# Router logits with the tokens' columns as the loaded operand, and the last two groups routed one slot sooner, in an adaLN block with linear attention and a mixture of experts

## What is computed

```python
h = layernorm(x) * (1 + ca) + sa
x = x + ga * attention(h)             # 16 heads of 16, phi = elu + 1, causal linear attention
h = layernorm(x) * (1 + cb) + sb      # sb, cb, gb: one row of 256 for each of the 4 batches

logits = h @ w_router.T               # 8 experts
gates = softmax(logits); two best experts for each token
position in the expert = running count over the tokens; at most 1280 are kept for each expert
hidden = silu(h @ w_gate.T)
y = sum over the two experts of gate * (hidden @ w_down[e].T)
x = x + gb * y
```

## Time and profile before

| what | value |
|---|---|
| median of 3 runs | 863.83 us (863.52 to 989.26) |
| profiled execution, its own time | 863.09 us |
| span from first to last instruction of it | 861.1 us |
| outside the span | 2.0 us |
| TensorE busy | 790.2 us, 92% |
| VectorE, ScalarE, GpSimd busy | 585.6, 488.7, 472.5 us |

### The profile page before, as it was taken

How to read it: one execution, slowest core, us unless ns; L and a number is a source line. 1 busy time by engine, 2 the same in 40 slices (tenths; PEclk the granted TensorE clock), 3 DMA queues, 4 the chain that set the end, 5 groups by cost and what they waited for, 6 DMA issues and landing times.

```text
span 861.1 us, 24360 instructions
## 1 busy us (share of the span) xinstructions
PE 790.2 (92%) x9388; PEld 647.2 (75%) x9388; DVE 585.6 (68%) x1753; ACT 488.7 (57%) x1001; POOL 472.5 (55%) x579
## 2 busy tenths in 40 slices
PE   5899999999999999999999999722999999999993
PEld 4676777777777777777777777511999999999993
DVE  4666677777776877867777767770566767767662
ACT  5656665766756756667657665421555555554541
POOL 2202345664664675665656645465356656656654
PEclk9999999999999999999999999955999999999997
DMA  5579913232332233323222212223466676677553
GB/s 195 175 229 284 310 19 125 84 91 100 84 114 90 86 111 95 83 97 71 66 86 64 52 50 58 48 78 120 102 155 130 135 167 133 146 158 156 122 91 37
DMA packets 71425, 99.00 MB, mean 115 GB/s; under 512 B 7810, under 2 KB 52866, under 8 KB 71320
## 3 DMA queue, kind: packets, MB, share of 16 engines
q1 hardware_dynamic: 38744, 53.93, 22.7%
q0 software_dynamic: 21760, 31.66, 16.9%
q10 hardware_dynamic: 10816, 11.96, 4.4%
HBM read 46.84 MB, written 63.36 MB: 128 GB/s over the span
## 4 chain that ended last, share of the span: by engine, by line
PE 73%; POOL 9%; issue 6%; ACT 6%; DVE 4%; DMA 2%; ACTq 0%; POOLq 0%; SPq 0%; DVEq 0%
PE SCW L1523 13%; PE PJ L1365 7%; PE SCW L1538 7%; PE MD L1538 6%; PE SCW L1305 6%; PE MD L1338 5%; PE SCW L1269 5%; PE PJ L1375 3%; PE SCW L1289 3%; POOL slot_rows L495 3%; PE MD L1279 3%; ACT N L671 2%; POOL rs L539 2%; POOL hT L532 2%; DVE Sm L919 2%
## 5 line engine op out<-in xcount | busy, mean ns | idle before, releaser
L495 POOL DMA_INDIRECT slot_rows<-Hrow,sloti x128 | 127.5, 996 | 141.4 <-PE SCW L1295 57.5
L919 DVE TENSOR_TENSOR Sm<-SCW,tri 128x1024 f32<-128x1024 f32 x128 | 150.8, 1220 | 71.5 <-PE SCW L1269 69.9
L601 POOL DMA_INDIRECT out<-EX,desti x80 | 128.2, 1602 | 31.8 <-issue 31.8
L1365 PE MATMUL PJ<-hT,w_qkv 128*128 128x512 f32 x384 | 109.8, 419 | 2.4 <-POOL hT L532 2.4
L1365 PEld LDWEIGHTS PJ<-hT,w_qkv 128*128 128x128 f32 x384 | 69.8, 190 | 25.5 <-issue 7.2
L671 ACT ACTIVATE N<-X,nb,rs 128x256 f32<-128x256 f32 x128 | 66.3, 591 | 27.4 <-POOL nb L541 27.4
L1305 PE MATMUL SCW<-Sm,VA 128*17 128x128 f32 x2048 | 80.6, 275 | 0.0
L667 ACT ACTIVATE EX<-PJ 128x512 f32<-128x512 f32 x64 | 37.9, 592 | 66.7 <-PE PJ L1365 66.7
L1269 PE MATMUL SCW<-QM,KT 32*128 32x256 f32 x1024 | 73.3, 400 | 0.8 <-ACT OTs L789 0.5
L1338 PE MATMUL MD<-w_og,ATs 128*128 128x256 f32 x256 | 72.4, 405 | 0.5 <-ACT ATs L778 0.5
L827 ACT ACTIVATE VA<-SCW 128x512 f32<-128x512 f32 x80 | 47.8, 598 | 41.0 <-PE SCW L1523 40.5
(11 more groups left out here) (189 smaller groups left out, 1767.1 us busy)
## 6 DMA issues: line engine op xcount, KB each, us to landing
Hrow<-slot_rows SPq DMA_DIRECT2D x32, 516.0 KB, 4.1
slot_rows<-erow ACTq DMA_DIRECT2D x1, 10400.0 KB, 46.6
X<-x SPq DMA_DIRECT2D x16, 512.0 KB, 5.6
out<-X SPq DMA_DIRECT2D x16, 512.0 KB, 2.9
Hrow<-mod_rows SPq DMA_DIRECT2D x16, 512.0 KB, 7.9
QT<-slot_rows SPq DMA_DIRECT2D x8, 516.0 KB, 3.7
slot_rows<-Hrow,sloti POOLq DMA_INDIRECT x128, 2.8
N<-wd SPq DMA_DIRECT2D x4, 512.0 KB, 4.2
```

Of the source, the lines that this page charges most:

```text
L495: pool.indirect_dma_start(xe, bass.IndirectOffsetOnAxis(sloti[:, par, k, t:t + 1], 0), Hrow[:, par, t, :], None, bounds_check=SLOTS - 1, o ...
L601: pool.indirect_dma_start(out, bass.IndirectOffsetOnAxis(desti[s % 2][:, a:a + 1], 0), Ys[s % 2][:, a, :], None, bounds_check=TOK - 1, oob ...
L919: dve.tensor_tensor(o.rearrange("p c (k w) -> p c k w", k=2), SCW[:, 2 * pair:2 * pair + 2, :].rearrange("p k (c w) -> p c k w", c=DC), tr ...
L1365: last = mm(PJ[m % 2][:], w_qkv[:, wp, cc, m * P:(m + 1) * P], hT[:, hp, cc, :], start=(cc + i == 0), stop=(cc == DC - 1 and i == len(SPLI ...
```

## The change

There are three parts.

- **Logits of all groups.** `h2T` becomes the loaded operand (128 x 128 for each of 4 tiles and 2 halves), and `w_r` with its 32 columns streams. The result has tokens on the partitions, so `logit_rows`, `lgT`, `lg` and both copies of ScalarE go away, and `choose` reads the logits from PSUM.
- **Group 14** has its statistics in slot 60, its normalisation in slot 61, its columns and logits in slot 62, `choose` in slot 63 and `place` in slot 64.
- **Group 15** is normalised in two pieces (three tiles, then one) and routed at once in a function `last_group`. In both groups the rows to send come from `h2T`: TensorE transposes it back (`rows_back`) and ScalarE copies it to `Hrow` (`rows_kept`), in place of VectorE's 16 scalings. The sends of GpSimd are listed anew.

The diff, cut (the same name `last_group` appears in several engines; `weights` is the block with the two `Exp` and the copy that stood at the end of ScalarE's slot; `columns_scaled` scales a range of columns as L745 did):

```diff
+        last_lg = KR[:, 0:GT * 32].rearrange("p (t w) -> p t w", t=GT)
+        last_pos = KR[:, 256:256 + GT * E].rearrange("p (t e) -> p t e", t=GT)
...
-            late = {TILES - 3: "pick", TILES - 2: "place", TILES - 1: "columns", TILES: "pick", TILES + 1: "place"}
+            late = {TILES - 3: "pick", TILES - 2: "place", TILES - 1: "pick", TILES: "place"}
             if n in late:
-                return (n + 1) // 4 - 2 if n != TILES + 1 else GROUPS - 2, late[n]
-            return n // 4 - 2, (("columns", "first", "second", "place")[n % 4] if n // 4 - 2 != GROUPS - 2 else None)
+                return GROUPS - 3 + (n - TILES + 3) // 2, late[n]
+            return n // 4 - 2, ("columns", "first", "second", "place")[n % 4]
...
+                    if g >= GROUPS - 2:
+                        pool.wait_ge(rows_out, 2 * (g - GROUPS + 2) + 2)
                     pool.tensor_tensor(idle[:, 5:6], mhalf[:, 0:1], mhalf[:, 0:1], ALU.add).then_inc(rested, 1)
-                    if g == GROUPS - 1:
-                        pool.wait_ge(last_rows, 1)
...
                     departure(GROUPS - 3)
-                    send_row(0, 0)
+                    send_row(0, 0, 1)
+                    pool.wait_ge(on_full, TILES - 1)
+                    send_row(0, 1, 1)
                     pool.wait_ge(knt_full, TILES)
-                    send_row(0, 1)
-                    pool.wait_ge(state_full, TILES)
-                    send_row(1, 0)
+                    send_row(1, 0, 1)
+                    pool.wait_ge(at_full, TILES - 1)
+                    send_row(1, 1, 1)
                     pool.wait_ge(sent[0], 128 * (GROUPS // 2 - 1))
                     number(GROUPS - 2)
+                    pool.wait_ge(state_full, TILES)
+                    send_row(2, 0, 1)
+                    pool.wait_ge(op_full, TILES - 1)
+                    send_row(2, 1, 1)
+                def last_deviations(t0, t1, part):
+
+                    ts = slice(t0, t1)
+                    pool.wait_ge(vpe2, GROUPS - 1 + part)
+                    pool.tensor_tensor(rs2[:, ts], vp2[:, ts], mhalf[:, ts], ALU.pow).then_inc(pow2, 1)
+                    pool.wait_ge(pow2, GROUPS - 1 + part)
+                    pool.tensor_tensor(nb2[:, ts], nm2[:, ts], rs2[:, ts], ALU.mult).then_inc(rstd2, 1)
+
                 if n == TILES:
+                    last_deviations(0, GT - 1, 1)
                     pool.wait_ge(on_full, TILES)
-                    send_row(1, 1)
-                    pool.wait_ge(at_full, TILES)
-                    send_row(2, 0)
-                    pool.wait_ge(op_full, TILES)
-                    send_row(2, 1)
-                if leaving and gn > GROUPS:
-                    send(2 * q)
-                    if q == 0:
-                        send(1)
+                    send_row(3, 0, 1)
+                    send_row(3, 1, 1)
+                    departure(GROUPS - 2)
+                    send_row(0, 0, 0)
+                    last_deviations(GT - 1, GT, 2)
+                    send_row(0, 1, 0)
+                    for t in range(1, GT):
+                        for k in range(2):
+                            send_row(t, k, 0)
+                    pool.wait_ge(sent[1], 128 * (GROUPS // 2 - 1))
+                    number(GROUPS - 1)
+                    departure(GROUPS - 1)
+                    for t in range(GT):
+                        for k in range(2):
+                            send_row(t, k, 1)
...
+                if q == 1 and gn == GROUPS - 1:
+                    deviations(rs2, vp2, nm2, nb2, vpe2, pow2, rstd2, G)
...
+            def last_norm(t):
+
+                act.wait_ge(rstd2, GROUPS - 1 + (1 if t < GT - 1 else 2))
+                act.wait_ge(h_lo, 2 * GROUPS)
+                normalise(N1[:, t, :], t, (GROUPS - 1) * GT + t, rs2, nb2, n2_ready)
+
+            def columns_scaled(cidx, cols, full):
+
+                act.wait_ge(h2t_full, full)
+                act.wait_ge(col2_done, 1)
+                act.activation(h2T[:, cidx, cols], PJ[cidx][:, cols], ACT.Identity,
+                               scale=saca2[:, DC + cidx:DC + cidx + 1],
+                               bias=saca2[:, cidx:cidx + 1]).then_inc(h2t_done, 1)
+
+            def rows_kept(g, half):
+
+                late = g - GROUPS + 2
+                act.wait_ge(sent[g % 2], 128 * (GROUPS // 2 - 1))
+                act.wait_ge(back_full, 2 * late + half + 1)
+                act.activation(Hrow[:, g % 2, 2 * half:2 * half + 2, 0:D],
+                               PJ[half * late][:].rearrange("p (t d) -> p t d", t=2), ACT.Copy).then_inc(rows_out, 1)
...
+            def last_group():
+
+                for t in (0, 1):
+                    last_norm(t)
+                act.wait_ge(at_full, TILES)
+                act.activation(ATs[:].rearrange("p c i -> p (c i)"), MA[:, 0:D], ACT.Copy).then_inc(at_done, 1)
+                last_norm(2)
+                act.wait_ge(lg_full, GROUPS - 1)
+                act.wait_ge(back_full, 2)
+                for cidx in range(DC):
+                    columns_scaled(cidx, slice(0, 3 * P), 2 * (GROUPS - 1) + cidx + 1)
+                last_norm(3)
+                for cidx in range(DC):
+                    columns_scaled(cidx, slice(3 * P, 4 * P), 2 * GROUPS + cidx + 1)
+                for half in range(2):
+                    rows_kept(GROUPS - 1, half)
+                weights(GROUPS - 1)
...
-                if routed and step in ("first", "pick"):
-                    act.wait_ge(lgt_full, g + 1)
-                    act.activation(lgT[:], PJ[1][:, 0:P], ACT.Copy).then_inc(lgt_done, 1)
...
-                if routed and step in ("first", "pick"):
-                    take(lg, lg_ps[:, :, 0:E], lg_full, g)
...
+                if n == TILES - 2:
+                    act.wait_ge(lg_full, GROUPS - 2)
+                    for cidx in range(DC):
+                        columns_scaled(cidx, slice(0, GW), 2 * (GROUPS - 2) + cidx + 1)
                 if n == TILES - 1:
-                    columns_out()
...
+                of = (last_lg if g == GROUPS - 1 else lg_ps)[:, :, 0:E]
+                if k > 0:
+                    dve.wait_ge(route, NR * g + k)
+                else:
+                    dve.wait_ge(lg_full, g + 1)
                 if k == 0:
-                    dve.wait_ge(taken, g + 1)
-                else:
-                    dve.wait_ge(route, NR * g + k)
-                if k == 0:
-                    done(dve.tensor_reduce(lmax[:], lg[:], AX_X, ALU.max))
+                    done(dve.tensor_reduce(lmax[:], of, AX_X, ALU.max))
                 elif k == 1:
-                    done(dve.tensor_tensor(lp[:], lg[:], wide(lmax[:]), ALU.subtract))
+                    done(dve.tensor_tensor(lp[:], of, wide(lmax[:]), ALU.subtract))
...
+            def last_deviations(t0, t1, part, between):
+
+                ts = slice(t0, t1)
+                dve.wait_ge(n2_ready, 4 * (GROUPS - 1))
+                dve.wait_ge(bn2, 4 * (GROUPS - 1) + t1)
+                for t in range(t0, t1):
+                    dve.bn_aggr(mv2[:, t, :], st2[:, t, :]).then_inc(ag2, 1)
+                between()
+                dve.wait_ge(ag2, 4 * (GROUPS - 1) + t1)
+                dve.tensor_scalar(nm2[:, ts].unsqueeze(2), mv2[:, ts, 0:1], -1.0, None, ALU.mult)
+                dve.tensor_scalar(vp2[:, ts].unsqueeze(2), mv2[:, ts, 1:2], LN_EPS, None, ALU.add).then_inc(vpe2, 1)
+
+            def last_group():
+
+                normalise_heads(TILES, lambda: None, lambda: None)
+                for k in range(9):
+                    place(GROUPS - 2, k)
+                add_out(TILES)
+                dve.wait_ge(x1_done, TILES)
+                row_stats(TILES - 1, GT - 1)
+                last_deviations(GT - 1, GT, 2, lambda: None)
+                for k in range(13):
+                    choose(GROUPS - 1, k)
+                for k in range(9):
+                    place(GROUPS - 1, k)
...
+                if n == TILES - 4:
+
+                    dve.wait_ge(x1_done, n)
+                    row_stats(n - 1, GT - 1)
+                    dve.wait_ge(bn2, n)
+                    ln_tail(st2, mv2, vp2, nm2, ag2, vpe2, GROUPS - 1)
+                if n == TILES - 1:
+                    dve.wait_ge(x1_done, n)
+                    row_stats(n - 1, 2)
+                    last_deviations(0, GT - 1, 1, between)
...
-                if n == TILES - 1:
-
-                    dve.wait_ge(mb_in, 32)
-                    dve.wait_ge(n2_ready, 4 * (GROUPS - 1))
-                    dve.wait_ge(sent[0], 128 * (GROUPS // 2 - 1))
-                    for t in range(GT):
-                        dve.tensor_tensor(Hrow[:, 0, t, 0:D], N2[:, t, :], MB[:, BATCH - 1, 2, :],
-                                          ALU.mult).then_inc(h2_scaled, 1)
-                    for t in range(GT):
-                        dve.wait_ge(h2_scaled, 4 * (GROUPS - 2) + t + 1)
```

(69 more changed lines are left out.)

145 lines of the change are left out of this document (52 added, 93 removed).

## The result

The changed kernel takes 879.08 us (median of 4 runs, 874.38 to 883.75), the kernel before 867.33 in the same comparison (4 runs, 863.52 to 989.26): ratio 1.0158, 95% interval 1.0114 to 1.0201, both formed without the disturbed run of before (989.26), which is why the ratio isn't that of the two medians. It is slower, by 1.1 to 2.0%: clear of no change by its interval, while the 2% that the forecast set as its bar lies at the very end of the interval. The profiled execution took 874.38 us, 11.29 more than that of before.

A forecast was written before the change was run, and what follows sets the result against it. TensorE was taken to bound stage one, and VectorE's small steps then GpSimd's sends the stretch between stages. The profiled 863.09 us plus 14.8 for stage one less 2.7 at the end gave 875.2 us, range 866 to 882.

The forecast's parts named there:

- The forecast's own case: Whole kernel: each group's logits cost +1.0 to +1.35 us, the end changes by -4 to -1; chance 0.58.
- Stage one: TensorE's full stretch: 14 groups at 1.17 us, less 1.6 absorbed, add 14.8 us (12.8 to 20.2).
- The pair of load and product: New logits on TensorE: 0.115 us for each of 16 pairs, 1.84 us a group.
- Rival A: New logits: loads hide, 25 to 60 ns a pair, total 860 us, not slower; chance 0.14.
- rival B: New logits: load and stream serial, 0.139 us a pair, 880.6 us, or 883.3 without end gain; chance 0.12.
- What is absorbed: Stage one: TensorE's waits for GpSimd's low part of `hT`, in 7 groups, absorb 1.6 us in all.
- `choose` reads PSUM, not `lg`: VectorE's `choose` in stage one: its 32 elements cost the same within some 0.05 us.
- Rival D: Stage one: ScalarE's removed copies release TensorE by up to 0.58 us a group, total 867.1; chance 0.07.
- Slot 62: TensorE gets eight transposes (1.1 us) and group 14's logits (1.84) from slot 63, 2.9 us in all.
- 3.2 us sooner: Between the stages: GpSimd's first send of group 14 can start at 567.3, before 570.53.
- The end's gain: Between the stages: group 14 is routed and sent sooner, its sends done about 579.1; gain 2.7 us.
- Rival C: Between the stages: group 15's routing or the wait for deviations replaces the sends, no gain, 877.9; chance 0.09.

The follow-up runs named there:

- Experiment 1: The kernel before with only the new form of the logits, in all 16 groups: 876.27 us, ratio 1.0128 to the kernel before.
- experiment 4: The changed kernel with 128, 96, 64 and 32 columns streamed for a group's four tiles instead of 32, groups 0 to 14: 876.83 us, ratio 1.0119.
- 3: The changed kernel with 8 router columns streamed for each load instead of 32, in groups 0 to 14: 878.0 us, ratio 1.0133.
- 5: The changed kernel with the store of group 15's `X` rows issued behind the first loads of stage two: 874.16 us, ratio 1.0105.
- 8: The changed kernel with that store late and group 15's gates held back until the last logits are done: 877.62 us, ratio 1.0145.
- 2: The changed kernel with the old logits in groups 0 to 14, so the new end alone: 865.0 us, ratio 0.9984 to the kernel before.
- 6: The changed kernel with old logits in groups 0 to 14 and the late store of group 15's `X` rows: 862.2 us, ratio 0.9966.
- 11: The changed kernel with old logits in groups 0 to 14, late store, and tile 63's deviations behind the 114th send: 862.6 us, ratio 0.999.
- 9: The changed kernel with eight small additions more on GpSimd ahead of the last two sends of group 13: 876.69 us, one run.
- 10: The changed kernel with the last send of group 13 moved behind the first send of group 14: 875.66 us, one run.
- 7: The changed kernel with tile 63's deviations on GpSimd ahead of group 14's first send, not behind it: 880.66 us, ratio 1.018.

## Why the prediction was right, and where two of its terms were not

The time forecast was 875.2 us for the profiled execution, which took 874.38; the median of the first comparison is 879.08, inside 866 to 882. The forecast's own case (a group +1.0 to +1.35) came true in stage one. In the end (-4 to -1) it did not. Stage one added 11.4 us where 14.8 was forecast, and the end gave back 0.1 where 2.7 was forecast: two misses of 3.4 and 2.6 us cancel. That the sum is right to 0.8 us is luck; the main cost and its size are not.

**The pair of load and product** was taken as 0.115 us and is 0.112 (0.111 and 0.113 with other streams). A group was forecast at 1.17 us with the transpose taken off. It is 1.13 in the routed slot, less 0.06 in the slot behind it, 1.07: 15.1 us for 14 groups, where 16.4 was forecast. Experiment 1 gives the same with nothing else changed. L1236 of the earlier trace rows, halved for the clock, gave 0.106; the loads' 0.83 ns a column of the earlier trace rows gave 107 ns. The Trainium skill, page "TensorE: Matmul & The Clock Gate", section "LDWEIGHTS (loading the stationary operand)", whose rule made it 1.71 us, is within 5% of the 1.79 measured. The Trainium skill, section "Back-to-back issue gap" of the same page, gives the 60 cycles, which made 0.4 us, for a product by itself and says that they count no load; here, with a load for each product, it was 1.78 us with 8 columns and 1.80 with up to 128.

**Rival A** (the loads hide) is refuted by the same rows, and **rival B** (load and stream in series) by experiment 4: in series, an average of 80 columns streamed would have taken longer than 32, by L1338's 1.04 ns a column some 0.05 us a pair, 0.8 us in 16. It took 0.01 more.

**What is absorbed** was mis-sized: 1.6 us forecast, 3.0 measured (3.74 less the transpose's 0.75); another 0.7 came by the start and by steps of chance. The step that failed is "it shows in 7 groups, six at 0.16 or 0.17 us as in the earlier trace rows and the first at 0.64". The mechanism and the six groups were right, but the wait really costs 0.43 us each. The seventh could not absorb anything: it stands ahead of the first routed logits and is still 0.64 us in the changed kernel. A row's idle time counts from the modelled end of the matmul before it, which lies well behind the time at which the next could have started: from the first piece to the next product it was 1.91 us before and is 1.50 after, 0.41 less for a wait shown as 0.16. The slots' distances give the true size. The rest, 0.42 us in three slots, is a case of "`choose` reads PSUM, not `lg`; its 32 elements cost the same within some 0.05 us": VectorE's second step got 0.46 us shorter there, as shown with the result.

**Rival D** (missing cover of ScalarE's copies) would have given back up to 0.58 us a group. The routed slots grow by 1.13, and the slots behind that hold neither the wait for `hT` nor `w_og` give back 0.05 or 0.06, which the transpose explains. Nothing is left for the copies.

**Slot 62** grew by 2.30 us, not 2.9; the first send of group 14 starts 31.74 us after the scores of slot 61, forecast 31.5 (567.3 - 535.76), before 34.77. So "3.2 us sooner" was 3.0. This part held. In experiments 3, 4, 5 and 8, with the same list on GpSimd, that send comes at 31.04 to 31.10: the changed kernel's execution has a gap of 0.64 us in front of the gate that they lack.

**The end's gain** was 2.7 us by forecast and 0.1 measured. The step that failed is "Now it is 0.99 for the first, 1.6 for the deviations with their waits, and seven at 0.97 + 0.30". From the first send to the row numbers of group 15 it took 592.99 - 578.90 = 14.09 us, not 11.8. The deviations with their wait cost 1.12 (1.6 forecast), the sends 1.28 each as forecast, and in addition there is the pause of 3.28 us. The hitch before the same send in the kernel before, 1.53 us less the usual 0.30, was part of the 11.3 us that I read, and I let it vanish in the new sum where I should have carried it. It did not vanish, it grew by 1.75. Why it is there isn't known (see below). **Rival C** had this price (2.7 us), and its place, but not its cause: the deviations came early enough (wait 0.27 us), and group 15 was routed 2.5 us before its turn, where 0.8 was forecast; counted from the first send of group 14 the routing was 0.6 us later than forecast and the sends 2.3.

With this, both halves stand apart (scores of slot 61 to stage two): before 62.01, new logits alone 62.61, new end alone 60.23, both 61.90. The new end is worth 1.8 us; the new logits of group 14, at the start of that stretch, take most of it back: 1.13 us by the scores of slot 63 (16.49 us behind those of slot 61, with the old logits 15.36). With experiments 3, 4, 5 and 8, where the stretch takes 61.44 to 61.52 us, both together leave 0.1 to 0.6 us of gain. The logits of groups 0 to 13 cost 11.4 more in front of it.

**Best version:** the new end with the old logits. It beats the changed kernel by over 1%. Against the kernel before, the path gives it 1.7 to 2.1 us, 0.2%, in all three executions (experiments 2, 6 and 11), but only one of the three ratios has an interval that leaves out 1 (experiment 6, 0.9938 to 0.9994), so by device time it isn't told from the kernel before.

**Still open:** why GpSimd pauses at the 114th send. It is neither of SyncE's transfers (5, 8), no place in the list as far as eight steps move it (9), not a group's first send (10), and no step of VectorE holds GpSimd off: in the changed kernel VectorE runs nothing from 580.07 to 584.51. Its size goes with what stands in front: 1.53 us behind a send that itself started after a gap of 0.16 (before and 1), 2.22 to 2.27 behind one that started after 0.54 or 0.56 (7, 11), 3.28 with the deviations between (all others). What happens in it was not seen, and whether it goes with the rows that are still on their way to memory was not tried.

## What to carry to other kernels

Turning a small product round changes which side is loaded: with as many pairs, 128 columns loaded for 32 made 0.112 us a pair out of 0.036, and making the stream shorter did not help. It also gave up the quarters of the output in which the old products lay, and the two were not told apart. An engine's real wait is read from the distance between the starts of fixed neighbours, slot against slot, not from the idle time behind a modelled end. When a sum replaces a measured stretch by its parts, carry its unexplained remainder along; a pause that isn't understood doesn't go because its neighbours moved.

## What was unexpected of the hardware

In all thirteen kernels GpSimd paused before the same indirect DMAs, with nothing to wait for in the profile: at the 53rd send (1.01 or 1.02 us, where the same send of most groups has 0.68 to 0.82), at the 114th (1.53 to 3.28, where 0.30 is usual behind a send and 0.54 behind a step) and at the 189th, in stage two (1.25, where 0.52 is usual). That the count fixes the place was tried at the 114th only. A smaller gap does not go by the count: 0.83 us at the 153rd in the changed kernel, it stands at the 151st (0.82) with the eight steps more of experiment 9, and the kernel before has 0.52 at both.

The other surprise is told with the result: a VectorE step of 128 x 32 elements took 0.59 us or 0.13 us beside the same GpSimd step, by where one of its inputs lay.
